# Linear attention and twelve experts on one core: pair jobs one or two places later, value halves just ahead of their use

## The reference

```python
xn = layernorm(x) * gamma + beta
w = sigmoid(xn @ Wx @ Ww + bw); k = xn @ Wk; v = xn @ Wv; r = sigmoid(xn @ Wr)
state = (1 - w_t)[..., None] * state + k_t[..., None] * v_t[..., None, :]
y_t = r_t @ state
x = layernorm(x + y @ Wo)
probs = softmax(x @ gate_w.T); top_w, top_i = top_k(probs, 2); weights normalised
x = layernorm(x + sum_e cw_e * ((silu(x @ w1_e.T) * (x @ w3_e.T)) @ w2_e.T))
```

## Time and profile before

| | us |
|---|---|
| runs | 790.75, 801.8, 802.55 |
| median | 801.8 |
| the profiled execution | 804.0 |
| its span | 802.1 |
| PE busy in it | 735.0 (92%) |
| DVE, ACT, POOL busy | 489.5, 347.2, 305.6 |
| chunk 0's first scores to the end of chunk 12 | 59.4 to 393.5 |
| chunks 13 to 15 and what follows, to the experts' first product | 393.5 to 483.9 |

### The profile page before, as it was taken

How to read it: one execution, slowest core, us unless ns; L and a number is a source line. 1 busy time by engine, 2 the same in 40 slices (tenths; PEclk the granted TensorE clock), 3 DMA queues, 4 the chain that set the end, 5 groups by cost and what they waited for, 6 DMA issues and landing times. The chain is left out here.

```text
span 802.1 us, 17861 instructions
## 1 busy us (share of the span) xinstructions
PE 735.0 (92%) x6197; PEld 537.9 (67%) x6198; DVE 489.5 (61%) x1102; ACT 347.2 (43%) x695; POOL 305.6 (38%) x336
## 2 busy tenths in 40 slices
PE   8998899999999999999988882799999999999994
PEld 3677587886878878778776761466666666666641
DVE  2845858768587686776876668244444444444467
ACT  3765645655456556576464111222222222222264
POOL 0447355454563545645521002043443443343310
PEclk9999999999999999999998566799999999999998
DMA  8722345245453454536310008144555665622765
GB/s 332 276 93 96 129 166 183 75 159 159 159 162 100 161 159 157 172 122 209 106 68 14 14 27 332 49 136 153 183 196 196 206 225 206 226 92 87 287 247 205
DMA packets 40123, 126.77 MB, mean 158 GB/s; under 512 B 4224, under 2 KB 4608, under 8 KB 38144
## 3 DMA queue, kind: packets, MB, share of 16 engines
q1 hardware_dynamic: 31024, 99.49, 35.5%
q0 software_dynamic: 6880, 22.55, 8.1%
q10 hardware_dynamic: 2160, 3.93, 1.4%
HBM read 81.13 MB, written 44.83 MB: 157 GB/s over the span
## 5 line engine op out<-in xcount | busy, mean ns | idle before, releaser
L1045 DVE COPY_PREDICATED ST<-msk,pS 128x256 f32<-128x256 uint8 x224 | 121.1, 569 | 77.8 <-issue 46.8
L717 POOL TENSOR_TENSOR piece_parts<-piece,piece_parts 128x1024 f16<-128x1024 f32 x48 | 103.8, 2163 | 114.8 <-ACT piece_parts L662 114.7
L1510 PE MATMUL pH<-ring,xgh 128*128 x344 | 104.0, 302 | 5.3 <-issue 2.8
L711 POOL TENSOR_TENSOR L<-L,AM 128x256 f32<-128x256 f32 x96 | 72.6, 757 | 83.6 <-ACT L L654 75.4
L1511 PE MATMUL pH<-ring,xgh 128*128 x344 | 103.7, 301 | 0.0
L1512 PE MATMUL pH<-ring,xgl 128*128 x344 | 103.6, 301 | 0.0
L382 PE MATMUL pS<-L 64*128 64x64 f32 x1536 | 102.5, 282 | 0.0
L382 PEld LDWEIGHTS pS<-L 64*128 64x128 f32 x1536 | 97.2, 199 | 0.0
L1822 POOL DMA_INDIRECT y_scratch<-ysb,sidx x43 | 42.8, 995 | 140.9 <-DVE ysb L1739 137.5
L1723 DVE TENSOR_TENSOR hid<-pH,sil 128x320 f32<-128x320 f32 x43 | 21.1, 491 | 118.5 <-ACT sil L1593 118.5
L695 DVE TENSOR_TENSOR L<-L,AM 128x256 f32<-128x256 f32 x96 | 63.7, 664 | 29.7 <-ACT L L641 27.8
(11 more groups left out here) (249 smaller groups left out, 1574.7 us busy)
## 6 DMA issues: line engine op xcount, KB each, us to landing
piece<-in_w_experts SPq DMA_DIRECT2D x48, 512.0 KB, 5.1
w_split_scratch<-piece_parts SPq DMA_DIRECT2D x48, 512.0 KB, 3.9
ring<-w_split_scratch SPq DMA_DIRECT2D x12, 2048.0 KB, 8.5
yin<-y_scratch SPq DMA_DIRECT2D x16, 512.0 KB, 12.9
out_x<-X SPq DMA_DIRECT2D x8, 512.0 KB, 2.8
x_scratch<-X ACTq DMA_DIRECT2D x15, 256.0 KB, 2.0
X<-in_x SPq DMA_DIRECT2D x2, 1536.0 KB, 18.3
X<-in_x SPq DMA_DIRECT2D x2, 512.0 KB, 6.5
```

Of the source, the lines that this page charges most:

```text
L711: g.tensor_tensor(next_kept(k, lv, 0), kept(key, k, lv, 0), by, ALU.mult).then_inc(k_dec, 1)
L717: g.tensor_tensor(piece_parts[buf][:, 1, :], piece[buf][:, :], piece_parts[buf][:, 0, :], ALU.subtract).then_inc(piece_lo, 1)
L1045: v.copy_predicated(out[:, :, :, 0 if lv == 0 else 1, :], msk[:, lv, :, :].rearrange(shape, m=m), pS[:, :, lv * S:(lv + 1) * S].rearrange( ...
L1510: pe.matmul(p[:, 0, 0:F], xgh[par][:, k, :], wh, start=(k == 0), stop=False)
```

## The change

Key half 2 (job 5) moves from the last slot of the odd chunk to the first of the even one; receptance follows a slot later; and the value halves of the pair before, (q-1, 8) and (q-1, 9), stand in the last slots, in the chunk ahead of the one that uses them. START loses (1,5) and (0,9). Jobs take their bank by their place in SEQUENCE and no longer by m. `apply_values` half 0 waits for its value half. Those of the last pair become units "value" 0 and 1 among the gating steps, in slot 5 of chunks 13 and 14; the third "gate" step moves from slot 6 of chunk 14 to slot 5, direct 12 and 13 each move by a place. Of the pieces, two instead of three belong to chunk 0 and four instead of three to chunk 1. Ahead of chunk 0: six products of zeros instead of three; ACT casts wh_r before the second root and normalisation; DVE takes the second statistics before low_x(0, 0); ACT casts wo before the first pieces, and POOL splits wo before them.

```diff
-START = [(0, 0), (0, 1), (0, 4), (0, 5), (1, 0), (1, 1), (0, 2), (0, 3), (0, 6), (0, 7), (0, 8), (0, 9)] + [(1, m) for m in range(2, 6)]
+START = [(0, 0), (0, 1), (0, 4), (0, 5), (1, 0), (1, 1), (0, 2), (0, 3), (0, 6), (0, 7), (0, 8), (1, 2), (1, 3), (1, 4)]
-FIRST = [[2], [3], [4], [5], []]
-SECOND = [[6], [7], [8], [9], []]
+FIRST = [[(0, 2)], [(0, 3)], [(0, 4)], [(-1, 8)]]
+SECOND = [[(0, 5)], [(0, 6)], [(0, 7)], [(-1, 9)]]
+SEQUENCE = list(START)
+for chunk_pair in range(1, NPAIR):
+    if chunk_pair > 1:
+        SEQUENCE += [(chunk_pair, 0), (chunk_pair, 1)] + [(chunk_pair + d, m) for slot in FIRST for d, m in slot]
+    SEQUENCE += [(chunk_pair + d, m) for slot in SECOND for d, m in slot]
-PIECES = [4 if n and n % 2 == 0 and n <= NT - 4 else 3 for n in range(NT - 2)] + [0, 0]
+PIECES = [2, 4] + [4 if n % 2 == 0 else 3 for n in range(2, NT - 2)] + [0, 0]
...
-GATE_SLOTS = {NT - 3: [[0, 1], [2, 3], [4], [5], [6, 7], [8], [9]], NT - 2: [[10], [11], [12, 13], [14], [15], [], [16]],
+GATE_SLOTS = {NT - 3: [[0, 1], [2, 3], [4], [5], [6, 7], [8, 9], [10]], NT - 2: [[11], [12], [13, 14], [15], [16], [17, 18], []],
...
         def order(q, m):
-            return START.index((q, m)) if isinstance(q, int) and (q, m) in START else q * JOBS + m
+            return SEQUENCE.index((q, m))
...
@@ tensor
+            def value(o, half, par):
+                tok = slice(half * P, (half + 1) * P)
+                for kt in range(KT):
+                    pe.matmul(o, xh[par][:, kt, tok], wh["v"][:, kt, :], start=(kt == 0), stop=False)
+                    pe.matmul(o, xh[par][:, kt, tok], wl["v"][:, kt, :], start=False, stop=False)
+                    i = pe.matmul(o, xl[par][:, kt, tok], wh["v"][:, kt, :], start=False, stop=(kt == KT - 1))
+                return i
...
             def apply_values(n, k, half):
                 pair, c = in_pair(k)
+                if half == 0 and n // 2 < NPAIR - 1:
+                    pe.wait_ge(a_out, done(n // 2, 8 + c))
+                if half == 0 and n // 2 == NPAIR - 1:
+                    pe.wait_ge(gate_out, taken("value", c))
...
             def gate_step(u):
+                elif kind == "value":
+                    t = value(pA[:, bank, :], i, (NPAIR - 1) % 2)
...
-            for i in range(3):
+            for i in range(6):
                 pe.matmul(pY[:, 0, :], state[:, 0, :], state[:, :, :].rearrange("p k t -> p (k t)"), start=True, stop=True)
...
@@ scalar
             high_x(0, 0)
+            high(1)
             root(1, 4)
             a.wait_ge(stat1, 6)
             normalise(1)
             for m in range(KT):
                 high_z(m)
-            high(1)
...
-            take(0, 8, 0)
             act_receptance(a, 0, 0, 3)
             act_receptance(a, 0, 0, 4)
+            take(0, 8, 0)
             act_receptance(a, 0, 0, 5)
-            take(0, 9, 0)
-            act_piece(a, 0, 0, 0)
-            take(1, 2, 1)
-            act_piece(a, 0, 0, 1)
             a.wait_ge(w_in[5], 32)
             a.copy(wo_h[:, 0:2, :], wo_stage[0]).then_inc(wo_hi, 1)
+            take(1, 2, 1)
+            a.copy(wo_h[:, 2:4, :], wo_stage[1]).then_inc(wo_hi, 1)
             take(1, 3, 1)
-            a.copy(wo_h[:, 2:4, :], wo_stage[1]).then_inc(wo_hi, 1)
+            act_piece(a, 0, 0, 0)
             take(1, 4, 1)
-            act_piece(a, 0, 0, 2)
-            take(1, 5, 1)
+            act_piece(a, 0, 0, 1)
@@ vector
+            part_stats(1)
             low_x(0, 0)
-            part_stats(1)
             part_terms(1)
@@ gpsimd
-            for t in range(PIECES[0]) if n == 0 else ():
-                pool_piece(g, n, k, t)
             for i in range(2):
                 g.wait_ge(wo_hi, i + 1)
                 g.tensor_tensor(wo_l[:, 2 * i:2 * i + 2, :], wo_stage[i], wo_h[:, 2 * i:2 * i + 2, :], ALU.subtract).then_inc(wo_lo, 1)
+            for t in range(PIECES[0]):
+                pool_piece(g, 0, 0, t)
```

More of the change, by code:

```diff
@@ L80, in needed @@
     kind, i = UNITS[u]
-    before = {"turn": 0, "gate": taken("turn", i * GROUP + GROUP - 1) if kind == "gate" else 0,
+    before = {"turn": 0, "value": 0, "gate": taken("turn", i * GROUP + GROUP - 1) if kind == "gate" else 0,
               "sum": taken("gate", i) if kind == "sum" else 0, "direct": taken("turn", i) if kind == "direct" else 0}[kind]
@@ L330, in _ @@
         def _(pe):
+            def value(o, half, par):
[5 more added lines that the diff above has]
+                return i
             def job(q, m, par):
-                bank = m % 2
                 at = order(q, m)
-                if not isinstance(at, int) or at >= 2:
+                bank, half = at % 2, m % 2
+                if at >= 2:
                     pe.wait_ge(a_out, at - 1)
@@ L350, in job @@
                         o = pA[:, bank, f * PAIR:(f + 1) * PAIR]
-                        cols = slice((2 * bank + f) * P, (2 * bank + f + 1) * P)
+                        cols = slice((2 * half + f) * P, (2 * half + f + 1) * P)
                         for kt in range(KT):
@@ L356, in job @@
                 else:
[L357 to L361, removed]
+                    i = value(pA[:, bank, :], half, par)
                 i.then_inc(a_full, 1)
@@ L491, in chunk @@
             def chunk(n, k, jobs=None):
-                q, par, slots = jobs or (None, None, [[]] * 5)
+                q, par, slots = jobs or (None, None, [[]] * 4)
                 def fill(s):
-                    for m in slots[s]:
-                        job(q, m, par)
+                    for d, m in slots[s]:
+                        job(q + d, m, (q + d) % 2)
                 def gating(s):
@@ L733, in take @@
             def take(q, m, par, n=None):
-                bank = m % 2
+                bank, half = order(q, m) % 2, m % 2
                 a.wait_ge(a_full, order(q, m) + 1)
-                if isinstance(q, int) and q == 1 and (m == 6 or m == 8):
+                if q == 1 and (m == 6 or m == 8):
                     a.wait_ge(wo_lo, 2)
@@ L755, in take @@
                     for f in range(2):
-                        t = 2 * bank + f
+                        t = 2 * half + f
                         i = a.activation(dec[par][:, :, t * P:(t + 1) * P],
@@ L760, in take @@
                 else:
-                    i = a.copy(val[par][:, bank, :], pA[:, bank, :])
+                    i = a.copy(val[par][:, half, :], pA[:, bank, :])
                 i.then_inc(a_out, 1)
@@ L804, in gate_take @@
                     ins = a.copy(xT[:, :, r * P:(r + 1) * P], pA[:, bank, :].rearrange("p (k t) -> p k t", k=KT))
+                elif kind == "value":
+                    ins = a.copy(val[(NPAIR - 1) % 2][:, i, :], pA[:, bank, :])
                 elif kind == "gate":
@@ L831, in fill @@
                 def fill(s):
-                    for m in slots[s]:
-                        take(q, m, par, n)
+                    for d, m in slots[s]:
+                        take(q + d, m, (q + d) % 2, n)
                 def gating(s):
@@ L922, in chunk @@
                 fill(3)
-                fill(4)
             a.sem_inc(st_used, 2)
```

11 lines of the change are left out of this document (5 added, 6 removed).

## The result

Over 20 runs of each, the changed kernel takes 789.14 us (786.95 to 791.32) where the one before takes 803.02 (790.75 to 805.11): a ratio of 0.9879, 95% interval 0.9854 to 0.9904. That is 1.2% faster, 13.9 us of medians. The forecast was 782.6 us, a gain of 19.2 us against the median of the runs shown then. The profiled execution took 791.1 us, span 789.2. The changed kernel was profiled twice more, with 790.23 and 791.0 us as medians (ratios 0.9869 and 0.9878).

A forecast was written before the change was run, and what follows sets the result against it. PE was taken to bound chunks 1 to 12 at full clock, with waits and half clock in the tail. Gains of 11.2 us at the start and 8.0 in the tail, 19.2 together, gave 782.6 us, range 775 to 794.

The forecast's parts named there:

- setup: Ahead of the jobs before chunk 0: more warm-up products and earlier wh_r cast gain 2.1 us, bounds 0.5 to 3.1.
- two jobs fewer: Ahead of chunk 0: PE is gapless, so dropping two jobs starts chunk 0's scores 5.2 us sooner.
- chunk 0: Chunk 0: wo split first and fewer pieces bring level 0, kbT and second mask earlier, gaining 3.9 us, bounds 0 to 6.8.
- chunks 1 to 12: Chunks 1 to 12: same ten jobs a pair, value half ready in time; gain 0, bounds -1 and +1.
- tail: Chunk 13 to the experts: filled PE gaps and full clock through chunk 14 gain 8.0 us, bounds -1 to 10.2.
- 1.3 of 4.7: Chunk 15: VectorE's waits for output products and second scores, 2.0 + 2.7 us, lacking a filler, credited with 1.3 us.
- B: Rival for the tail: the clock falls there all the same, tail gives 2, time 788.6 us; chance 0.22.
- C: Rival for chunk 0: it keeps its waits because piece loads hold ScalarE and the levels, 786.5 us; chance 0.15.
- D: Rival: the clock falls in the tail and chunk 0 keeps its waits, both together, 792.5 us; chance 0.08.
- E: Rival, slower: late value half on ScalarE makes every even chunk's apply wait, 805.4 us at 12 us each; chance 0.03.

The follow-up runs named there:

- experiment 2: Changed kernel with ScalarE taking the second root before the cast of wh_r, not behind it: 785.63 us, ratio 0.9810 to the kernel before.
- experiment 4: Changed kernel with chunk 0's pieces as before, three ahead of wo's halves, and three for chunk 1: 796.97 us, ratio 0.9965 to the kernel before.
- experiment 5: The kernel of experiment 2 with the fourth piece of chunk 1 moved to chunk 13: 784.41 us, ratio 0.9807 to the kernel before.
- experiment 8: Changed kernel with the last pair's value halves one slot later, behind the second applies of chunks 13 and 14: 794.48 us, ratio 0.9925 to the kernel before.
- experiment 7: Changed kernel plus 12 unread products of 512 columns ahead of chunk 15's first apply: 787.03 us, ratio 0.9832 to the kernel before.
- experiment 9: Changed kernel with experiments 5 and 7 together: 782.16 us; second kernel adds 10 unread products ahead of chunk 15's second apply: 781.33; another adds 36 before the experts: 780.48.

## Why the prediction was wrong

The sign was right; the size was off by 6.3 us in the profiled execution (791.1 against 784.8). 5.0 of these lie at the start, 1.35 in the tail. The step that failed is the setup: 2.1 us were forecast, and none came. What each term of the sum gave, in us gained against the profile before:

| term | forecast | after | again | third |
|---|---|---|---|---|
| setup | 2.1 | 0.2 | -0.3 | -0.5 |
| two jobs fewer | 5.2 | 3.7 | 5.2 | 3.5 |
| chunk 0 | 3.9 | 2.3 | 4.9 | 5.1 |
| chunks 1 to 12 | 0 | 0.0 | -1.7 | -3.4 |
| tail | 8.0 | 6.65 | 6.5 | 6.6 |

- *The setup, 2.1 (bounds 0.5 to 3.1).* Below the lower bound in all three profiles. The prediction followed ACT alone ("one ScalarE chain is behind both"). What it left out is that an earlier cast of wh_r also starts GpSimd's 4.3 us sooner, on top of DVE's `nmr`, for which ACT's normalisation waits. The clock at 9 us did stay full, and the weights' products began at full rate (8.66); the time was lost again behind them. Without the collision (experiment 2) the step gives 2.9.
- *Two jobs fewer, 5.2.* The jobs went, PE stayed gapless, and the second profile has all 5.2. In the first PE ran at 0.93 of the clock there (1.6 us lost), in the third it has the half clock from 34 us. The reason given was incomplete: by experiment 4 the 5.2 are worth nothing without the new order of pieces, since the first apply of chunk 0 hung on GpSimd's chain. The prediction added them to chunk 0's 3.9 as if independent.
- *Chunk 0, 3.9.* The order was right: level 0 at 59.5, 6.0 us sooner though 2.5 later than forecast, kbT in time. Without a fall of the clock in it the chunk gained more than forecast, 4.9 and 5.1; the first profile has 6.8 us of half clock there, for which the sum had no term.
- *Chunks 1 to 12, 0 (within 1).* 305.68 us in the first profile, but by luck: chunk 0 was so slow that kbT was nearly in time. In the other two, 307.35 and 309.06, chunk 1 waited 2.5 and 2.2 us for kbT, outside the bound (the 309.06 has the fall at 89 us too). The fourth piece that the change puts into chunk 1 holds DVE's last decay (2.03 us, not 0.17) and with it GpSimd's level 0; experiment 5 takes that away. The prediction weighed the loads of that piece, not its GpSimd half beside DVE.
- *The tail, 8.0.* 6.65. Both gaps are filled and the clock is full through chunk 14, as forecast; experiment 8 puts the gaps back and loses 3.5. What was mis-sized is the "1.3 of 4.7" for chunk 15: the wait of 2.0 for output products did go, but the foreseen idle time ahead of its first apply lowered the clock for the last scores, whose wait grew by 2.0, and a wait of 1.7 for `rstd` was new. Experiment 7 shows 4.0 us to be had there.
- *The rivals.* B (the clock falls in the tail all the same) gives 788.6, close to what was measured, but that is luck: 409.6 to 445 is at 1.00, and the tail gained 6.65 where B has 2 (a figure for which the prediction shows no working). C (chunk 0 keeps its waits, 786.5) had the place nearly right, the start, but not the cause: the wait for kbT went. D needs both. E did not come: no apply waits for its value half.

The Trainium skill, SBUF — State Buffer, "SBUF: two separate sides", says that a VectorE operation with two SBUF inputs and a GpSimd one that reads SBUF take one shared pair of ports as a lock, and that the one that comes second stands still until the first has ended. The trace agrees to 0.02 us twice: `nmr` ends at 25.63 with GpSimd's 25.61, the last decay at 82.85 with its 82.83. The prediction did not apply that rule to the instructions that the change brings side by side.

The falls of the clock are the part that stays partly open. Over the 14 profiles of this case PE's idle times and the half clock behind them go together like this:

| idle time of PE, by place | profiles | with half clock in it or within 2.3 us behind |
|---|---|---|
| 1.63 us, before the second transposes of the setup | 9 | 6 |
| 0.25 to 0.31 us, same place (experiments 2, 5, 9) | 5 | 0 |
| 1.13 to 1.15 us, before chunk 0's first apply | 11 | 2 |
| 2.2 to 2.5 us, before chunk 1's output products | 5 | 4 |
| 0.8 to 1.6 us, same place | 9 | 0 |
| 2.7 us, before chunk 15's first apply | 7 | 7 |
| the same, filled with unread products | 4 | 0 |

So at three of the four places the wait that is left on PE cost more than its length in most executions, and every fall ahead of chunk 13 stands in an idle time of PE or within 2.3 us behind one. But the same wait is followed by half clock in one execution and not in the next, and at least three falls have no idle time near them (403 us above, 465 us in the kernel before, 432 us in experiment 9's second kernel). Why, no run here shows. In the three profiles of the changed kernel the falls ahead of chunk 13 cost between nothing and some 5 us of PE work.

## What to carry to other kernels

When an operation is moved forward, follow the engine that it releases and not only the one that it stands on: a long GpSimd operation that begins sooner can hold a 0.2 us VectorE operation, and through it the chain that was to gain. Work taken off an engine that looks gapless pays only if that engine ends the stage; ask which chain would be late next, and don't add two gains of one stage. And put useful or even unread products into an idle time of TensorE only ahead of work that others wait for: it took 4.0 us off the tail at chunk 15's scores (2.9 in the medians) and nothing off the experts' part. Profile a kernel more than once before a stretch of half clock is put down to its order of work.

## What the runs showed of the hardware that was not expected

- A VectorE product of two columns takes 0.16 us alone and 3.83 beside a GpSimd subtraction of 2048 columns; the same with the 8-column decay, 0.17 and 2.03.
- The granted clock can fall behind idle times of PE as short as 2.2 to 2.7 us, and PE is then busy 100% while it is low (0.57 over 34 to 38 us and over 89 to 93). With the idle time shortened or filled the half clock behind it did not come in any profile, at three places (the table above).
- It can also fall with no idle time near: at 403.3 us in the second profile, after 10.5 us of PE without a pause, and at 465.3 in the kernel before, after 21.8 us of it. Where the falls come changes from execution to execution of one kernel.
- A gap does not decide it either: 2.37 us idle ahead of the same apply was followed by half clock in the kernel before and by full clock in experiment 8. The Trainium skill, TensorE: Matmul & The Clock Gate, "HAM oscillation — how this bites in real kernels", explains such falls by idle gaps; experiment 7 agrees with it (2.73 us idle filled, clock full), the falls without a pause do not.
